# Attention's score banks as a third pair for the pair scores, with Gelu inputs made during selection and xn made on GpSimd

## The reference, cut to what matters

```python
x = x + attention(layernorm(x))          # 16 heads of 8 sharing one k and v, causal, T = 256
x = x + experts(layernorm(x))            # x: (16, 256, 128), float32

def experts(x):                          # 8 heads, 32 keys a side, 64 wide, TOPK = 16
    xn = rmsnorm(x) * gamma
    q = xn @ wq.T                        # two halves per head
    sim = einsum(q, keys)                # (half, token, head, 32)
    sx, sy = top_k(sim[0], 16), top_k(sim[1], 16)
    scores, pk = top_k(sx[:, None] + sy[None, :], 16)
    h = gelu(xn @ table_down[indices]) * softmax(scores)
    return sum(h * table_up[indices])
```

## Time and profile before

| | us |
|---|---|
| median of 3 runs | 1212.75 (1209.47 to 1215.9) |
| profiled execution | 1214.8 |
| its span | 1213.0 |
| VectorE busy | 992.3 (82%) |
| PE busy | 881.6 (73%) |
| ACT busy | 713.9 (59%) |
| GpSimd busy | 607.3 (50%) |
| mean granted TensorE clock | 0.788 of full |

### The profile page before, as it was taken

One profiled execution on the slowest core, in us unless ns is written; L12 is line 12 of the kernel. 1 busy time (PEld: TensorE's weight loads), 2 busy tenths in 40 slices (PEclk: granted clock), 3 DMA queues, 4 the chain that ended last, 5 costly groups with the idle time before them and its releaser, 6 DMA issues.

```text
span 1213.0 us, 20292 instructions
## 1 busy us (share of the span) xinstructions
PE 881.6 (73%) x5298; PEld 451.2 (37%) x5298; DVE 992.3 (82%) x4082; ACT 713.9 (59%) x993; POOL 607.3 (50%) x339
## 2 busy tenths in 40 slices
PE   4779687785867678686867868586786858677454
PEld 3234243342524334252433425253442525243232
DVE  2146897888979888888988889898888889887887
ACT  1436656575656657565665756566575656557353
POOL 1011845638184564818366481836548183653731
PEclk9976868696878969687787969878796977879665
DMA  5010102001010100101010010102011010100000
GB/s 137 1 30 1 30 2 35 0 12 22 5 29 0 33 0 16 18 5 29 0 33 0 18 16 5 29 0 33 0 20 14 5 29 0 29 1 5 1 5 5
DMA packets 36938, 19.72 MB, mean 16 GB/s; under 512 B 3632, under 2 KB 36528, under 8 KB 36720
## 3 DMA queue, kind: packets, MB, share of 16 engines
q1 hardware_dynamic: 36912, 19.42, 8.7%
HBM read 13.64 MB, written 5.24 MB: 16 GB/s over the span
## 4 chain that ended last, share of the span: by engine, by line
PE 38%; DVE 38%; issue 12%; ACT 9%; DMA 1%; DVEq 1%; SPq 0%; ACTq 0%
DVE prob L858 10%; PE score L1126 8%; ACT prob L581 5%; PE att L1053 5%; PE misc L1145 4%; PE att L1055 4%; DVE cand L801 3%; DVE late_scores L714 3%; DVE gated_t L879 3%; DVE left L784 3%; PE misc L1095 2%; PE misc L1075 2%; PE att L1023 2%; PE score L1102 2%; DVE y_t L729 2%
## 5 line engine op out<-in xcount | busy, mean ns | idle before, releaser
L398 POOL TENSOR_TENSOR acc<-acc,prob 128x1024 f32<-128x1024 f32 x186 | 438.5, 2357 | 14.1 <-DVE prob L858 1.4
L858 DVE SCALAR_TENSOR_TENSOR prob<-score,cut,prob 128x1024 f32<-128x1024 f32 x256 | 323.8, 1280 | 112.8 <-ACT prob L581 111.9
L581 ACT ACTIVATE prob<-score,neg_lse,unit 128x1024 f32<-128x1024 f32 x256 | 304.7, 1203 | 161.9 <-PE score L1126 121.5
L1126 PE MATMUL score<-sel,pieces_t 128*128 128x512 f16 x512 | 185.6, 451 | 110.3 <-DVE prob L858 109.9
L398 POOL TENSOR_TENSOR acc<-prob 128x1024 f32<-128x1024 f32 x31 | 73.1, 2357 | 224.3 <-DVE prob L858 224.3
L1023 PE MATMUL att<-k_stack,q_stack 48*128 48x256 bf16 (+1 forms) x512 | 108.2, 329 | 31.1 <-ACT halves L494 31.1
L511 ACT ACTIVATE probs<-att 128x512 f32<-128x512 f32 x192 | 109.6, 596 | 35.6 <-PE att L1055 34.2
L1126 PEld LDWEIGHTS score<-sel,pieces_t 128*128 128x128 f16 x512 | 39.9, 107 | 219.7 <-DVE prob L858 195.9
L1102 PE MATMUL score<-xn_t,wdt 128*128 128x256 f32 x256 | 80.3, 469 | 39.4 <-DVE gated_t L879 39.4
L352 POOL TENSOR_TENSOR rstd<-ln_tmp,half_neg 128x2 f32<-128x2 f32 x16 | 11.6, 725 | 179.8 <-DVE ln_tmp L694 179.8
L494 ACT ACTIVATE late_scores<-att 128x512 bf16<-128x512 f32 x128 | 76.4, 597 | 34.5 <-PE att L1026 34.5
(11 more groups left out here) (109 smaller groups left out, 1428.3 us busy)
## 6 DMA issues: line engine op xcount, KB each, us to landing
q_stack<-q_scratch SPq DMA_DIRECT2D x96, 64.0 KB
q_scratch<-qk_piece SPq DMA_DIRECT2D x16, 192.0 KB, 2.4
xin<-x SPq DMA_DIRECT2D x16, 128.0 KB, 5.4
xres<-x SPq DMA_DIRECT2D x16, 128.0 KB, 2.2
out<-fin SPq DMA_DIRECT2D x16, 128.0 KB, 1.8
k_stack<-qk_piece SPq DMA_DIRECT2D x96, 4.0 KB
prob<-consts SPq DMA_DIRECT2D x1, 1216.0 KB, 6.5
prob<-wq SPq DMA_DIRECT2D x1, 512.0 KB, 5.1
```

Of the source, the lines that this page charges most:

```text
L398: eng.tensor_tensor(acc[:, j, :], so_far, prob[:, j * FH + h, :], ALU.add).then_inc(acc_added, 1)
L581: eng.activation(prob[:, g, :], score[g % 2][:, :], ACT.Exp, bias=neg_lse[:, j, h:h + 1], scale=unit[:, :]).then_inc(prob_made, 1)
L858: eng.scalar_tensor_tensor(prob[:, g, :], score[g % 2][:, :], cut[:, j, h:h + 1], prob[:, g, :], ALU.is_ge, ALU.mult).then_inc(prob_masked, 1)
L1126: ins = eng.matmul(score[g % 2][:, cols], pieces_t[:, j, h, :], sel[:, cols], start=True, stop=True)
```

## The change

`score` gets a third pair of banks, and the two attention banks become its halves; `misc[1]` takes the projection. Pair score g uses pair g % 3 and waits for the mask of head g - 3; head 2 waits for attention's last exponential. Gelu's input is made per tile instead of per four chunks, both times in `score[2]`: tile 0's after the maxima's scores, tile 1's after ACT has read tile 0's. Gelu of tile 0 needs only the first `gate`. Attention's scores wait for the second Gelu, and the maxima's scores for the mask of head 14 of the batch before. `make_xn` goes from VectorE to GpSimd behind `scale`, in one function; GpSimd reaches it behind five adds and waits there for the statistics of x2. VectorE's order changes: both gates earlier, `finish` ahead of the second `select_pairs`, `qk_remainder` ahead of the masks, `log_sum_exp` after four masks, `make_y` after six, `make_x2` after eight. In the diff below `make_xn` is on GpSimd, `activate` on ACT and the rest on PE.

```diff
-        score = [ctx.enter_context(nc.psum_tensor(f"score{n}", [P, EXPERTS], FP32)) for n in range(2)]
-        att = [ctx.enter_context(nc.psum_tensor(f"att{n}", [P, BANK], FP32)) for n in range(2)]
+        score = [ctx.enter_context(nc.psum_tensor(f"score{n}", [P, EXPERTS], FP32)) for n in range(BUFS)]
+        att = [score[2][:, n * BANK:(n + 1) * BANK] for n in range(2)]
...
+            def make_xn(b):
                 eng.wait_ge(ln2_step, every(ln2_step, b))
                 if later(b):
                     eng.wait_ge(xn_made, at(xn_made, b, 0))
+                if later(b):
+                    eng.wait_ge(xn_tp, at(xn_tp, b, 0))
                 eng.tensor_tensor(scale2[:, :], bounded[:, :], half_neg[:, :], ALU.pow).then_inc(scale2_made, 1)
+                value = held(eng, every(scale2_made, b))
+                eng.wait_ge(setup_pool, 1)
+                eng.wait_ge(scale2_made, value)
+                for j in range(TILES):
+                    eng.tensor_scalar(xn[:, j, :], x2[:, j, :], mv2[:, j, 0:1], scale2[:, j:j + 1],
+                                      ALU.subtract, ALU.mult).then_inc(xn_made, 1)
...
+            def activate(b, j):
+                if j == 0:
+                    eng.preload_act_table_set("gelu_and_others")
+                eng.wait_ge(hidden, at(hidden, b, j + 1))
+                if later(b):
+                    eng.wait_ge(gated, at(gated, b - 1, j + 1))
+                eng.activation(act_t[:, :, j * P:(j + 1) * P], score[2][:, :].rearrange("p (c t) -> p c t", t=P),
+                               ACT.Gelu).then_inc(act_made, 1)
...
             def scores_for_probs(b, u):
                 if u < 2:
-                    eng.wait_ge(max_kept, every(max_kept, b))
+                    if later(b):
+                        eng.wait_ge(act_made, every(act_made, b - 1))
...
+            def hidden_units(b, j, a):
+                if j == 1:
+                    eng.wait_ge(act_made, at(act_made, b, 1))
+                elif a:
+                    eng.wait_ge(max_kept, every(max_kept, b + 1))
+                for c in range(CH):
+                    ins = eng.matmul(score[2][:, c * P:(c + 1) * P], wdt[:, c * P:(c + 1) * P],
+                                     xn_t[:, j * P:(j + 1) * P], start=True, stop=True)
...
-                    eng.wait_ge(prob_masked, at(prob_masked, b, g - 1))
+                elif g == 2 and a:
+                    eng.wait_ge(att_probs, every(att_probs, b + 1))
+                else:
+                    eng.wait_ge(prob_masked, at(prob_masked, b, g - 2))
-                    ins = eng.matmul(score[g % 2][:, cols], pieces_t[:, j, h, :], sel[:, cols],
+                    ins = eng.matmul(score[g % BUFS][:, cols], pieces_t[:, j, h, :], sel[:, cols],
```

More of the change, by code:

```diff
@@ L34 @@
 MAX_STEPS = 12
+BUFS = 3
 def later(batch):
@@ L946, in iteration @@
                 if f:
-                    mask(i, 0, 0)
-                    mask(i, 0, 1)
+                    select_pairs(i, 1)
                 if p:
@@ L951, in iteration @@
                 if f:
+                    mask(i, 0, 0)
+                    mask(i, 0, 1)
                     sum_best(i, 1)
-                    for h in range(2, FH):
-                        mask(i, 0, h)
+                    mask(i, 0, 2)
+                    mask(i, 0, 3)
                     log_sum_exp(i, 1)
+                    mask(i, 0, 4)
+                    mask(i, 0, 5)
                 if a:
@@ L958, in iteration @@
                 if f:
-                    mask(i, 1, 0)
+                    mask(i, 0, 6)
+                    mask(i, 0, 7)
                 if a:
@@ L962, in iteration @@
                 if f:
-                    mask(i, 1, 1)
-                if a:
-                    make_xn(i + 1)
-                if f:
+                    mask(i, 1, 0)
                     if not a:
+                        mask(i, 1, 1)
                         add_late_head(1)
-                    for h in range(2, FH):
+                    for h in range(1 if a else 2, FH):
                         mask(i, 1, h)
```

189 lines of the change are left out of this document (87 added, 102 removed).

## The result

The changed kernel takes 1171.05 us in the median of four runs (1159.3 to 1171.67), the kernel before 1211.94 in its four beside them: a ratio of 0.964, 95% interval 0.957 to 0.970. Forecast were 1131 us, in a range of 1080 to 1188. The direction is right and the size is too large: 41 us came where 80 were forecast. The profiled execution of the changed kernel took 1171.67 us, its span 1169.9.

The account below looks back on a forecast made before the run. VectorE leads without being full: its masks wait for ACT's exponentials, and it waits for GpSimd at sums. A batch takes 39.8 + 25.7 = 65.5 us; 88.2 + 15 x 65.5 + 60 = 1131 us, range 1080 to 1188.

Parts of the forecast that it names:

- M to S: From the start of masking (M) to the start of the next selection (S): 28.7 us, before 37.3.
- the L849 wait: VectorE's L849 during masking, reading two SBUF tensors under a GpSimd add: 1.3 us more than now.
- the last of the four waits: Towards the end of masking, from ACT's and PE's other work among exponentials and scores: 1.2 us of 4.1.
- xn on GpSimd: The two xn operations behind GpSimd's `pow`: 0.35 us each, estimated from adds at 2.3 ns a column.
- S to C: From selection's start to the end of the first tile's candidate sums (C), which wait for GpSimd; C = M + 39.8 taken.
- The two cases: End of the first tile's sums: C = M + 38.5, or M + 41.0 if S slips by over 0.5 us.
- Rival 1: Each of the five candidate sums waits for one GpSimd instruction: C = M + 43.3, 1183 us; chance 0.15.
- C to M: From the end of the first tile's candidate sums to the start of masking: 24.5 to 27.0 us, 25.7 taken.
- The wait of `finish`: Between candidate sums and masking: 1 to 3 us as before, with select_pairs behind it ending before L460.
- rival 3: The third pair's gain is lost in waits on `act_made` and `att_probs`, 5.3 us of new waits: 1213 us; chance 0.05.
- rival 4: xn slow on GpSimd, deciding from 3.2 us an operation; at 4 us each the kernel takes 1240 us; chance 0.08.
- The sum: Whole span: 88.2 us to the first C, 15 batches of 65.5, 60 behind the last C: 1131 us.

Follow-up runs that it names:

- two_pairs: The changed kernel with pair scores on two bank pairs instead of three, all else as changed: 1225.23 us, ratio 1.012.
- short_adds: The changed kernel with GpSimd's last three adds a batch on 16 of 1024 columns, so not computing the reference: 1082.26 us, ratio 0.893.
- warm: The changed kernel with the four transposes of the second tile's sum done four times over, ahead of the maxima's transpose: 1153.53 us, ratio 0.951.
- xn_dve: The changed kernel with xn made on VectorE again, all else as changed: 1173.88 us, ratio 0.970.
- only_xn: The kernel before with xn on GpSimd and nothing else changed: 1181.98 us, ratio 0.976.
- pe3_xn_dve: pe3 with xn back on VectorE: 1150.03 us, ratio 0.952.
- pe3: The changed kernel with three of the second tile's eight heads summed on TensorE instead of GpSimd, whole sum computed: 1105.08 us, ratio 0.914.
- keys_first: The changed kernel with second selection buffers; VectorE selects both tiles' keys, folds the maxima, then makes the sums; ACT's Gelu goes earlier: 1258.72 us, ratio 1.039.

## Why the prediction was right, and where it was not

- **What bounds the kernel.** Right: the masks' waits for ACT, and GpSimd's chain as what "has to be watched". two_pairs shows the first, short_adds the second. The weight was wrong: the chain was treated as a correction to the masks' gain, and it is what takes most of it. VectorE's masks wait 4.3 us a batch for ACT (68.7 / 16), where under 4 was forecast.
- **M to S, 28.7 us.** Measured 30.1. VectorE's work there was right (25.9 with the L849 wait, 25.1 measured), and so was that wait: the operation takes 1.45 to 1.62 us in every batch but the last, 0.22 where nothing holds it, so 1.2 to 1.4 where 1.3 was taken. The mis-sized term is the last of the four waits, "1.2 us towards the end": the masks of (1,4) to (1,7) waited 0.58, 1.49, 0.35 and 0.33 us, 2.75 together. 0.8 us of VectorE's work that did not come hid a part of that.
- **xn on GpSimd, 0.35 us each.** Measured 0.80, all 32 of them between 0.795 and 0.802 us, inside the bounds of 0 and 1.16 but far from the value taken. The slope of 2.3 ns a column was taken from adds and put on another operation. Adds go on shrinking (0.61 us for 256 columns, 0.25 for 16 in short_adds), so an add of 128 would lie between these, and it is the subtract-multiply with its two scalar columns that costs more, not the narrow shape. It made GpSimd's chain 0.9 us longer, with the `pow` at M + 17.4 (forecast 17.6).
- **S to C.** The two cases were right, and the choice of a mean was not. The forecast said that a slip of S by over 0.5 us gives C = M + 41.0; S slipped by 1.4, and C was M + 41.5, with the end of the add that was named (M + 41.3, forecast M + 40.8). Taking 39.8 between the two cost 1.7 of the 2.4 us a batch, the largest single part of the miss. Where the outcome is one of two steps, the value between them is one that can't come.
- **Rival 1** (every sum waits, C = M + 43.3, 1183 us) did not come: the sums end with GpSimd's second to last add, not its last. But its time is nearer to the result than the forecast's. The Trainium skill, SBUF — State Buffer, section "Who interferes with whom", says that the shared pair is an exclusive lock, and that the order of issue decides who blocks; that the two queues alternate one for one was the prediction's strict reading of it. The trace agrees that the sums are held, and not with the strict reading: the five took 5.8 us, which is less than three adds.
- **C to M, 25.7 us (24.5 to 27.0).** Measured 26.3 in the mean and 27.7 in the batch shown. The second half of the Gelu input was bounded by 1.95 and 3.9 us, and it took 1.95 to 3.62, 2.9 in the mean. So attention's exponentials start at C + 15.3 in the mean (14.2 to 15.9 in 13 batches), the middle of the forecast's C + 14.4 to 16.3. The mis-sized term is the one behind them: from there to the leading piece of q and k the forecast had 8.8 to 9.4 us. It is 8.9 in the five batches in which the first tile's expert output takes 1.95 us, and 10.4 to 11.9 in the eight in which it takes 2.87 to 3.62, at a granted clock of 0.50 to 0.66. The forecast counted 0.8 to 1.4 us for that output, and warm, where it is back at 1.95 in most batches, gives 1.1 us of C to M back.
- **The wait of `finish`, "1 to 3 us, but select_pairs behind it ends before L460 does".** It was 3.06 us a batch (49.0 / 16), and select_pairs no longer ended first: L892 at 588.32, then selection and the remainder up to 593.09 with no gap. But this wait is not alone at the end of C to M: ACT's L469 ends 0.03 us ahead of the remainder in every batch, so both chains end together, both behind TensorE's expert output.
- **The third pair, 5.3 us of new waits needed for rival 3**: it is worth 3.3 us of period and the whole direction of the result; without it the new order is slower than the kernel before.
- **GpSimd slow at xn (rival 4)**: 0.80 us is far from the 3.2 at which it decides.
- **By the rule of the GPSIMD Engine Reference** of the Trainium skill, section "4.1 Engine selection" (elementwise work belongs on VectorE), the move would lose. The section has the factor of two for operations with two inputs and calls GpSimd roughly line-rate with one. `xn` reads one tensor. With the other engine idle the trace agrees with the rule, and by more than a factor of two: the pair takes 0.60 us on VectorE in the prologue and 1.58 on GpSimd. That makes a loss of 1.0 us; the prediction's 0.4 does not follow from its rows, since twice 0.60 is 1.2 and a loss of 0.6. But beside GpSimd's adds the pair took 3.30 us on VectorE in xn_dve, so these rows spoke against the rule; and as the kernel stood, the whole gain of the move went into GpSimd's chain and TensorE's clock, and nothing of it was left. It pays where GpSimd's end leaves room: 2.4% in the kernel before (only_xn), and 45 us between pe3_xn_dve and pe3.
- **The sum.** First C 89.4 (88.2), 15 periods of 67.9 (65.5), 61.7 behind the last C (60): 1.2 + 36 + 1.7 = 39 us over.

What stays open: why S came 1.4 us late in the masks of (1,4) to (1,7) was read from the timeline and not tried; what the other 1.5 of the 2.6 us are by which C to M grew; and whether the fold ahead of the sums helps once its gate is ahead of it.

## What to carry to other kernels

An engine that is busy for half the span can still set the time, by where its chain ends: ask of each move not only what it frees on the full engine, but which chain it lengthens and what waits for the end of that one. Two parts of a change that draw on the same slack don't add up, so measure each alone and both together, and measure the part again once the slack is there (xn: 0 us, then 45). And work put into TensorE's idle stretches pays twice where it comes off an engine whose chain bounds: the other chain ends sooner, and in pe3 TensorE's own granted clock rose from 0.781 to 0.896.

## What was not expected of the hardware

- 336 repeated transposes, whose results nobody needs, made the kernel 17.5 us faster; what rose with them is the granted clock, from 0.82 to 0.89 from C to M. The same 16 records of float32 matmuls take 3.62 us at a granted clock of 0.50 and 1.95 at 1.00. The idle time ahead does not settle which one comes: behind 3.22 us of it they took 1.95 in one batch of the changed kernel, and behind 1.93 us 3.33 in one of warm.
- GpSimd's subtract-multiply of 128 columns takes 0.80 us, though an add of 256 columns takes 0.61, and one of 16 columns 0.25. The price goes by the operation and not by the columns alone.
- An operation of VectorE with two SBUF inputs is held by GpSimd in bf16 as in float32: one step of the fold took 3.26 us in keys_first, and 1.23 elsewhere.
- A transpose written as a float32 matmul with the identity accumulates in PSUM, at about twice the price of a transpose: 24 blocks in 5.62 us, 0.23 each, against 0.115 to 0.13 (3.67 / 32, 1.04 / 8). Three heads moved that way still took 66 us off the kernel.
